# Attention and FFN block on one core: the order of the prologue, and the values matmuls of full-width steps in two halves

## The reference, cut to what matters

```python
sim = jnp.einsum('bhid,bhjd->bhij', q, k)
sim = sim + jnp.transpose(bias, (2, 0, 1)) * SCALE
sim = sim + causal
attn = jax.nn.softmax(sim, axis=-1)
out = jnp.einsum('bhij,bhjd->bhid', attn, v)
```

## Time and profile before

| | us |
|---|---|
| median of 3 runs (lowest to highest) | 344.32 (344.03 to 344.61) |
| the profiled execution | 342.63 |
| its span | 340.8 |
| outside the span | 1.83 |
| TensorE busy | 286.3 |
| VectorE busy | 272.6 |
| ScalarE busy | 190.3 |
| GpSimd busy | 92.0 |

### The profile page before, as it was taken

The page is one execution under the profiler, slowest core; times in us unless marked ns, Lnnn a source line. Parts: engine busy times, 40 slices in busy tenths (PEclk is TensorE's granted clock), DMA queues, the critical chain, the costliest instruction groups (busy, mean ns, idle before and its releaser), DMA issues.

```text
span 340.8 us, 8308 instructions
## 1 busy us (share of the span) xinstructions
PE 286.3 (84%) x3224; PEld 129.0 (38%) x3224; DVE 272.6 (80%) x967; ACT 190.3 (56%) x264; POOL 92.0 (27%) x138
## 2 busy tenths in 40 slices
PE   8492987769998989998898999889899988999880
PEld 4151342222343344334334334423432443367650
DVE  5653556989899888988888989888899957838894
ACT  2433544386558556755766674685575468843230
POOL 6109999602020220201022022001200001615351
PEclk9967698969999999999999999999999999999997
DMA  7475417001010120102022222114221002000022
GB/s 217 131 205 145 132 38 236 17 2 38 21 56 4 56 56 3 53 7 57 0 57 56 34 64 55 35 25 87 56 34 26 9 14 37 4 4 13 0 63 62
DMA packets 16263, 18.80 MB, mean 55 GB/s; under 512 B 4576, under 2 KB 11872, under 8 KB 16096
## 3 DMA queue, kind: packets, MB, share of 16 engines
q1 hardware_dynamic: 13168, 12.10, 14.6%
q0 software_dynamic: 2400, 3.45, 3.5%
q10 hardware_dynamic: 656, 2.73, 2.7%
HBM read 11.81 MB, written 4.23 MB: 47 GB/s over the span
## 4 chain that ended last, share of the span: by engine, by line
PE 52%; DVE 22%; ACT 11%; issue 6%; DMA 4%; POOL 3%; SPq 1%; DVEq 0%; POOLq 0%
PE ps L1174 15%; PE ps L1130 12%; ACT PT L743 9%; DVE FM L883 8%; PE ps L1145 8%; PE ps L1162 7%; DVE junk L890 4%; PE ps L1052 3%; DMA qk_scratch<-QS 2%; PE ps L1207 2%; DVE st L947 2%; DVE U L1000 1%; PE ps L1116 1%; PE ps L1077 1%; DVE xnT L913 1%
## 5 line engine op out<-in xcount | busy, mean ns | idle before, releaser
L743 ACT ACTIVATE PT<-ps 128x1024 f32<-128x1024 f32 (+1 forms) x192 | 144.7, 814 | 92.2 <-PE ps L1162 87.3
L883 DVE TENSOR_REDUCE FM<-ps 128x1 f32<-128x512 f32 (+2 forms) x192 | 109.1, 616 | 12.8 <-PE ps L1130 12.3
L890 DVE CUSTOM_DVE_ANT_0 junk<-ps,NBH 128x256 bf16<-128x256 f32 (+1 forms) x256 | 90.2, 399 | 23.5 <-PE ps L1130 23.5
L1130 PE MATMUL ps<-KA,QA 56*128 56x256 bf16 (+3 forms) x544 | 96.5, 288 | 14.7 <-DVE FM L883 7.4
L1145 PE MATMUL ps<-QA,KA 58*128 58x512 bf16 (+3 forms) x384 | 77.7, 333 | 17.6 <-ACT PT L743 14.6
L1174 PE MATMUL ps<-PT,VG 128*16 128x512 f32 (+3 forms) x768 | 86.1, 493 | 0.1
L1130 PEld LDWEIGHTS ps<-KA,QA 56*128 56x128 bf16 x544 | 33.3, 95 | 99.8 <-DVE FM L883 42.1
L420 POOL DMA_DIRECT2D KA<-qk_scratch x30 | 16.4, 550 | 163.3 <-PE ps L1162 151.9
L1145 PEld LDWEIGHTS ps<-QA,KA 58*128 58x128 bf16 x384 | 24.8, 94 | 37.4 <-ACT PT L743 30.4
L1162 PE MATMUL ps<-TT,flb 128*32 128x176 f16 (+4 forms) x1152 | 38.4, 243 | 0.0
L1162 PEld LDWEIGHTS ps<-TT,flb 128*32 128x32 bf16 x1152 | 21.3, 96 | 17.1 <-issue 15.5
(11 more groups left out here) (98 smaller groups left out, 256.2 us busy)
## 6 DMA issues: line engine op xcount, KB each, us to landing
QA<-qk_scratch SPq DMA_DIRECT2D x64, 48.0 KB
KA<-qk_scratch POOLq DMA_DIRECT2D x30, 96.0 KB, 2.6
qk_scratch<-QS SPq DMA_DIRECT2D x12, 128.0 KB
qk_scratch<-QS SPq DMA_DIRECT2D x8, 192.0 KB
X<-in_x SPq DMA_DIRECT2D x4, 256.0 KB, 5.1
PT<-fr_scratch ACTq DMA_DIRECT2D x1, 1024.0 KB, 5.6
out<-U SPq DMA_DIRECT2D x4, 256.0 KB, 2.3
OT<-f_scratch ACTq DMA_DIRECT2D x2, 480.0 KB, 8.3
```

The source lines that it names most:

```text
L743: nc.scalar.activation(PT[:, s % 3, 2 * q:2 * q + 2, off:off + w], ST[:, q, :, off:off + w], ACT.Exp).then_inc(s_exp, 1)
L883: nc.vector.tensor_reduce(FM[:, ib, heads[0]:heads[-1] + 1:2, piece], bank[:, 0:w * len(heads)].rearrange("p (h n) -> p h n", n=w), AX.X, ...
L890: last = nc.vector.tensor_tensor_reduce(junk[:, n % NSM, i, 0:w], bank[:, i * w:(i + 1) * w], nb[:, h, 256 - w:256], 1.0, NEG, ALU.add, AL ...
L1130: last = nc.tensor.matmul(SM[:, n % NSM, i * w + j - j0:i * w + j - j0 + nj], QA[r0:r0 + KS, p, ib // 4, q, (ib % 4) * 128:(ib % 4 + 1) * ...
```

## The change

- **Bias tables.** `task_f` is split: the reversed table first, its load `rev` issued by SyncE as soon as it is stored; the other table later, its conversion to float16 moved from VectorE to GpSimd, its stores and the TL loads later on SyncE, behind the loads of group 0.
- **Stores.** Query and key stores have semaphores of their own; key parts 1 and 2 of chunk 0 are issued by ScalarE; the third query part of chunk 1 moves from VectorE to GpSimd.
- **TensorE's order.** 10 fillers first (waiting for OV's clearing), F (reversed), T, F (other), Q, K, 5 fillers, V of half 0, 4 fillers, flips 0 to 3, T, Q, K, V of half 1, flips 4 to 7. The banks change with it.
- **Batch 1.** Its eight tasks stand at positions 7, 9, 10, 12, 13, 15, 16, 18 of the unit order, Q and K apart. OWN0 is 21; unit "m 0" of group 0 moves two places forward; the 12 fillers before the first scores go. ScalarE writes Q and K of batch 1 once, GpSimd makes the first part too. The bias copy `copy_tt(0)` is last on ScalarE. GpSimd takes both deviations of batch 1 at once.
- **Values.** A full-width step's values become two halves of 256 columns, with the first unit of the place "after the values" between them.

```diff
+def order_of(g):
+    ks = list(range(NU - 1))
+    if g == 0:
+        ks.remove(M0)
+        ks.insert(M0_FIRST, M0)
+    return ks
+M0_FIRST = SPLIT0 + 3
...
-T_AT = {2: 0, 8: 1}
-QK_AT = {4: 0, 10: 1}
-V_AT = {13: 0, 15: 1}
+BATCH1_AT = {7: ("T", 0), 9: ("Q", 0), 10: ("K", 0), 12: ("V", 0), 13: ("T", 1), 15: ("Q", 1), 16: ("K", 1), 18: ("V", 1)}
-OWN0 = 17
+OWN0 = 21
...
             sp.wait_ge(s_f, 1)
             sp.dma_start(bass.AP(fr_d, 0, [[H, 128], [128 * H, XC], [1, H]]), Fr[:, :, :]).then_inc(s_fst[0], 16)
+            sp.wait_ge(s_fst[0], 16)
+            sp.dma_start(rev[:, :], bass.AP(fr_d, 0, [[H, 128], [1, 256 * H]])).then_inc(s_rev, 16)
+            sp.wait_ge(s_q1, 2)
+            store_keys(sp, 0, 0, 0)
+            store(0, 0, 0)
             sp.wait_ge(s_f, 2)
...
-            key_part(0, 0)
-            key_part(0, 1)
-            store(0, 0, 0)
-            key_part(0, 2)
-            sp.wait_ge(s_qst[0][0], STORED)
+            sp.wait_ge(s_qst[0][0][0], STORED_Q)
             load_q(sp, 0, 0, 0)
...
             load_q(sp, 0, 0, 1)
+            sp.wait_ge(s_fst[1], 32)
+            for part in range(2):
+                sp.dma_start(TL[64 * part:64 * part + 64, :],
+                             bass.AP(f16_d, part * BW * H, [[H, 64], [1, NEARU * H]])).then_inc(s_tl, 16)
...
+            pool.wait_ge(s_ff, 1)
+            nc.gpsimd.tensor_copy(F16[:, 0, :, :], Ff[:, :, :]).then_inc(s_p3, 1)
...
+            queries_lo(0)
             pool.wait_ge(s_zero, 3)
-            pool.wait_ge(s_qst[0][0], STORED)
+            pool.wait_ge(s_p2, 1)
+            pool.wait_ge(s_qst[0][0][1], STORED_K)
             load_k(pool, 0, 0, 0, s_ldk)
-            pool.wait_ge(s_p2, 1)
+            queries_lo(1)
+            second_batch_deviation()
             second_batch_norm(2)
             second_batch_norm(3)
...
+            act.wait_ge(s_mid, 2)
+            store_keys(act, 0, 0, 1)
+            act.wait_ge(s_q3[0][1], 1)
+            store_keys(act, 0, 0, 2)
+            copy_nbh(0)
+            copy_nbh(1)
             turned(0, 1)
-            first_parts(0, 1)
-            for i in NBH_ACT:
+            copy_nbh(2)
+            first_parts(1)
+            for half in range(2):
+                copy_v(0, half)
+            for i in NBH_ACT[3:]:
                 copy_nbh(i)
...
             load_k(act, 0, 0, 1)
-            first_parts(1, 0)
+            whole(0)
+            copy_v(1, 0)
             turned(1, 1)
+            whole(1)
+            copy_v(1, 1)
             act.wait_ge(s_tl, 32)
             copy_tt(0)
-            first_parts(1, 1)
-            copy_v(1)
...
             pe.wait_ge(s_idle, 1)
-            keep_busy(5, 5)
+            pe.wait_ge(s_ov, 2)
+            keep_busy(7, 10)
             pe.wait_ge(s_tab, 16)
-            task_f()
-            keep_busy(5, 2)
+            task_f(1)
             pe.wait_ge(s_early, 16)
             task_t(0, 0)
-            task_qks(0, 0)
-            task_t(0, 1)
-            task_qks(0, 1)
-            pe.wait_ge(s_f, 2)
-            pe.wait_ge(s_ov, 2)
-            pe.wait_ge(s_cst, 2)
+            task_f(0)
+            for qk in range(2):
+                task_qk(0, 0, qk)
+            keep_busy(7, 5)
+            pe.wait_ge(s_mid, 1)
+            task_v(0, 0)
+            keep_busy(7, 4)
+            pe.wait_ge(s_cst, 1)
+            pe.wait_ge(s_ff, 1)
             pe.wait_ge(s_rev, 16)
             for i in range(4):
                 task_flip(i)
...
-            def values(g, p, s):
+            def values(g, p, s, between):
...
-                for h in range(HG):
-                    last = nc.tensor.matmul(OV[32 * h:32 * h + 2 * HD, off:off + w], VG[:, jb, g, h, :],
-                                            PT[:, s % 3, h, off:off + w], start=(jb == 0),
-                                            stop=(jb == 4 * ic + 3), skip_group_check=True)
+                cuts = [(off, w)] if w < IC else [(0, IC // 2), (IC // 2, IC // 2)]
+                for i, (c0, n) in enumerate(cuts):
+                    for h in range(HG):
+                        last = nc.tensor.matmul(OV[32 * h:32 * h + 2 * HD, c0:c0 + n], VG[:, jb, g, h, :],
+                                                PT[:, s % 3, h, c0:c0 + n], start=(jb == 0 and i == 0),
+                                                stop=(jb == 4 * ic + 3), skip_group_check=True)
+                    if i + 1 < len(cuts):
+                        between()
...
-                    values(g, p, s)
-                    s_units_at(s, 2)
+                    early = 1 if step_cols(*STEPS[s])[1] == IC else 0
+                    values(g, p, s, lambda: s_units_at(s, 2, 0, early))
+                    s_units_at(s, 2, early)
...
-            for k in JOBS[:JOBS.index(OWN0)]:
+            for n, k in enumerate(order_of(0)[:OWN0]):
+                if n in BATCH1_AT:
+                    second_batch(*BATCH1_AT[n])
...
             nc.tensor.matmul(ps[0:64, 0, 0:64], flb[:, 0:64], flb[:, 0:64], start=True, stop=True).then_inc(s_pv, 3)
-            keep_busy(1, 12)
             pe.wait_ge(s_tt, 1)
...
-NBH_ACT, NBH_DVE = (0, 2, 4, 5, 6, 7), (1, 3)
+NBH_ACT, NBH_DVE = (0, 1, 2, 4, 5, 6), (3, 7)
```

More of the change, by code:

```diff
@@ L124, in stream @@
     for g in range(G):
-        for k in range(NU - 1):
+        for k in order_of(g):
             if g and k == M1_BEFORE:
@@ L360, in build @@
         s_nbh = sem("s_nbh")
-        s_qst = [[sem(f"s_qst{b}{c}") for c in range(2)] for b in range(B)]
+        s_qst = [[[sem(f"s_qst{b}{c}{x}") for x in "qk"] for c in range(2)] for b in range(B)]
         s_late = sem("s_late")
@@ L863, in _ @@
             norm(1)
-            for k in range(2, 4):
-                stats0(k)
-            for i in NBH_DVE:
-                copy_nbh(i)
+            copy_nbh(NBH_DVE[0])
+            stats0(3)
+            nc.vector.tensor_copy(idb[:, :], idf[:, :]).then_inc(s_cst, 1)
             for qk in range(2):
                 split(1, qk)
+            copy_nbh(NBH_DVE[1])
             def unit(g, p, k):
@@ L1035, in _, with task_f @@
         def _(pe):
-            def task_f():
-                for k in range(2 * XC):
-                    last = nc.tensor.matmul(ps[:, BANK["F", 0, 0], k * H:(k + 1) * H],
-                                            oh_s[:, k // XC, (k % XC) * 128:(k % XC + 1) * 128], emb_s[:, :],
+            def task_f(a):
+                for c in range(XC):
+                    last = nc.tensor.matmul(ps[:, BANK["F", 0, a], c * H:(c + 1) * H],
+                                            oh_s[:, a, c * 128:(c + 1) * 128], emb_s[:, :],
                                             start=True, stop=True)
@@ L1095, in _ @@
             pe.wait_ge(s_mid, 2)
-            task_v(0, 0)
+            task_t(0, 1)
+            for qk in range(2):
+                task_qk(0, 1, qk)
             task_v(0, 1)
@@ L1226, in group, with s_units_at @@
             def group(g, p, load, last=False, first=False):
-                def s_units_at(s, pos):
-                    for later, k in (SLOTS0 if first else SLOTS).get((s, pos), []):
+                def s_units_at(s, pos, i0=0, i1=None):
+                    for later, k in (SLOTS0 if first else SLOTS).get((s, pos), [])[i0:i1]:
                         if later and last:
@@ L1307, in stage0_tasks @@
 def stage0_tasks():
[L1309 removed]
+    order = [("F", 0, 1), ("T", 0, 0), ("F", 0, 0), ("Q", 0, 0), ("K", 0, 0), ("V", 0, 0),
+             ("T", 0, 1), ("Q", 0, 1), ("K", 0, 1), ("V", 0, 1)]
     for half in range(2):
[L1311 to L1317 removed]
+        order += [(kind, 1, half) for kind in "TQKV"]
+    bank = {("F", 0, 1): 6, ("F", 0, 0): 5}
+    bank.update({("T", 0, 0): 0, ("T", 0, 1): 3, ("Q", 0, 0): 2, ("K", 0, 0): 3, ("Q", 0, 1): 4,
                  ("K", 0, 1): 5, ("V", 0, 0): 2, ("V", 0, 1): 3,
```

183 lines of the change are left out of this document (90 added, 93 removed).

## The result

The changed kernel takes 340.81 us in the median of 4 runs (337.59 to 341.20), beside 344.17 for the kernel before on the same chip (342.29 to 344.61). The ratio is 0.9882, with a 95% interval of 0.9840 to 0.9924: faster by 1.2%, some 4 us by the ratio (3.4 by the medians), where 12 were forecast. The profiled execution took 341.2 us, its span 339.4.

What follows compares the result with a forecast made beforehand. Prologue held to be bound by waits, chiefly an 8.36 us key and query landing, steady groups by TensorE's chain with excursions through VectorE. -10.0 (A) and -2.0 (B) take 344.32 to 332.3 us; range 324.5 to 340.

Steps and rivals of the forecast that it cites:

- part B: Values of full-width steps in two halves with a unit between: -0.3 us per group, -2 us in all, bounds +8 and -13.
- part A: The prologue, up to the end of group 0: reordered loads and units save 10.0 us, bounds 3 and 14.
- below 2.5: Sign that the forecast is right: VectorE's idle time in a steady group of 28.9 us falls under 2.5 us.
- Step (1): Start of the units: key parts land at 20.0 us instead of 25.35, units start at 25.3; -5.4 us, bounds -1.3 and -6.9.
- The other gate: Start of the units: the bias tile is ready near 24.5 us, just hidden behind the loads; 1 us of delay shows.
- Step (2): First unit to first scores: 13.0 us of VectorE work and 4.6 idle, 17.6 in all, bounds 15 and 20.4.
- only part of A arrives: Rival, 20%: in the prologue a queue takes back what the DMA gave; A -4, B about 0, 340 us.
- The normalised tile comes 4 to 5 us earlier: Units to first scores: GpSimd's batch 1 tile comes earlier with the key load, so TensorE's 2.1 us wait goes.
- the fillers' 2.70 us: Units to first scores: the 12 filler matmuls are removed and their 2.70 us go.
- Step (3): Rest of group 0: VectorE work falls by 2.6 us, a low clock may cost some; -1.8 us, bounds -4 and +1.
- takes about twice that: Rest of group 0: without fillers, one full-width block of 0.99 us takes about twice as long at the low clock.
- slower: Rival, 8%: in steps 5 to 8 the unit between values waits for its bank; at 2.0 us per group, +13, 345.5 us.

Runs made afterwards that it cites:

- e1: The changed kernel with the values of full-width steps in one piece again, so the prologue part alone: 341.19 us, ratio 0.9916 to the kernel before.
- e4: The changed kernel with values in halves but no unit between them, the units behind as before: 341.76 us, ratio 0.9899 to the kernel before.
- e12: The changed kernel itself, unaltered, measured once more on one chip beside later runs: 339.75 us, ratio 0.9859 to the kernel before.
- e11: e8 with two fillers ahead of each of nine units in step 2 of group 0: 331.95 us, ratio 0.9620 to the kernel before.
- e3: The changed kernel with SyncE's TL loads, and what stands behind them, waiting for the chunk 1 keys and queries: 337.56 us, ratio 0.9783 to the kernel before.
- e9: The changed kernel, order of loads left alone, with both sets of fillers of e8: 339.17 us, ratio 0.9845 to the kernel before.
- e8: e5 with the fillers of both e6 and e7: 331.17 us, ratio 0.9591 to the kernel before.
- e6: e5 with 10 filler matmuls ahead of the first unit and 2 ahead of each of units 1 to 6: 332.81 us, ratio 0.9670.
- e7: e5 with 8 filler matmuls ahead of the first scores: 333.00 us, ratio 0.9651 to the kernel before.
- e5: e3 with the maximum row sent ahead of group 1's first query loads, and GpSimd's key loads moved behind batch 1's splits: 335.87 us, ratio 0.9724.
- e10: e8 with the values in one piece, the edit of e1: 334.57 us, ratio 0.9714 to the kernel before.

## Why the prediction was wrong

The direction was right (faster, 90%) and so was part B. The size of part A was wrong by 7 us (2.9 in e1, where 10 had been forecast, just outside its own bounds of 3 to 14), and 340.81 lies outside the range, though only just above it.

**Part B**, forecast -0.3 us per group. It is -0.43: 28.74 for 29.17, and five periods between the same output copies (107.16 to 250.86 against 106.72 to 252.55) give 2.1 us. The turn back from a unit costs 0.1 (0.32 for 0.22), as put, and the mechanism was the one named: ScalarE's exponentials start earlier once the unit does, and VectorE's gap closes in part. Part of the gap stays (0.18 here); the idle time in a group is 2.59 us, just missing the "below 2.5". The Trainium skill's rule that a change of the tiling mode drains TensorE (TensorEngine Tiling (Array Packing), Key Properties) bears on the turns alone: the trace shows their price and not what they consist of, and e4, which cuts without a unit between, costs nothing.

**Step (1)**, units at 25.3 us, forecast -5.4. The landing of the key parts fell from 8.36 to 5.00 us (4.4 in e12), where 4.26 had been put. But the part was ready at 16.60 instead of 15.68: Q and K start at 10.12, X having landed after 4.17 us and the other table (1.46 us) standing ahead of them, and they took 3.78 us in spite of the ten fillers. Units start at 27.55, and between 25.4 and 27.6 in all profiles with this prologue but that of e11 (29.53). The other gate was near, as said: the bias tile is ready at 25.11, and in e3 it releases the first unit. So 3 to 5 of the 5.4 came.

**Step (2)**, 17.6 us from units to first scores, is the step that failed: it took 24.1 us (26.6 in e12). VectorE's work was 13.11 as forecast (13.0), so the idle time was mis-sized, 11 us against 4.6. Three terms of it:

- "The change puts the two loads of the diagonal bias (480 KB each) behind everything of group 0" is true of SyncE's queue alone. The key load of chunk 1 is ScalarE's, and ScalarE comes to it 0.75 us after SyncE is past. I had read the order of one queue as the order of the loads. It costs a landing of 7.12 us where e3 shows 2.5 or less, and, by e3, 2 to 3 us of the time; and by e9 the fillers give nothing that can be told before it is mended. The rival "only part of A arrives" (20%), with 4 us left of A and 340 us in all, came nearest, though its B was put at nothing. It named GpSimd's norm behind the key load, which is one half of this (next point), and not ScalarE's key load beside the TL loads.
- "The normalised tile comes 4 to 5 us earlier": it comes 1.5 earlier (31.70 for 33.22, the start of its transpose), since GpSimd passes its wait for the key parts at 22.14 instead of 20.0, and the operation added ahead of the norm costs 1.17. This is what makes ScalarE late for its key load; e9 shows that being 0.8 us earlier would not have been enough.
- The clock. Only the rest of group 0 had a term for it. The first half's Q and K of batch 1 take 2.05 and 2.08 us as before at the low level, and the second half's 1.95 and 1.13, where the earlier trace rows has both in 1.96. In e8 each of the four takes 1.10 to 1.13. The forecast counted the fillers' 2.70 us as gained, and nothing for the clock that they had kept up; on the mended order, e8 puts that at 4.6 us and e6 and e7 at 2 to 3 each.

That the bias copy shows by about 1 us before the first scores came true (1.55).

**Step (3)**, -1.8. "Its VectorE work falls by the same 2.6" came true (-2.4), yet the stretch to the row's transfer shrank by 0.5. The mean clock over it is 0.62; with eight fillers back ahead of the scores (e7), first scores to first output copy fall from 23.5 us (e5) to 20.9. That a full-width block at the low clock "takes about twice that" was about the right price (half a block, eight records, takes 1.05 us at 59.60 and 0.62 at 145.46), and was counted at one block where it holds for most of 54 to 62 us and 68 to 80 us.

**The size of the whole** was not out of reach: e8, with the two queues ordered and the fillers in, takes 331.17 us, where 332.3 was forecast, and e10, its prologue without part B, is worth 9.9 us where part A was put at 10.0. That the sizes agree is in part luck: the forecast had counted the fillers as time saved, and e8 has 30 of them. It had priced the change that was meant and not the one that was made.

A slip beside this: the rival *slower* has 345.5 "with A at -12". The forecast's A is -10, and 344.3 - 12 + 13 is 345.3; with A at -10 it is 347.3. Its sign and chance do not hang on it.

What stays open: the clock term of the changed kernel is shown by adding fillers, not by a run at another clock; what makes the keys land late, the 960 KB alone or also the loads of group 1 issued behind them, is not parted; and the 3 us between the first scores and the output copy of e7 and e6 (20.9 and 23.9) were not looked into by engine.

## What to carry to other kernels

When a big load is moved later, write down every queue's issues with their expected times, not only those of its own queue: a small load that another engine issues at about the same time shares its way with it, and landed 5 us later here, which cost 2 to 3 us of the kernel. To issue it a little earlier is no cure: 0.07 us ahead it was as late (e9). Put a wait in front of the big load on the thing that it must not overtake, and put small transfers on the critical path ahead of the loads of the next stage. Fillers in the stretches where TensorE waits paid here only after the wait that comes last there was gone (e8 against e9), and where their own time was idle anyway (e8 against e11). A unit of work for a second engine that stands between two long blocks can be put into the middle of one, when its bank is free there; the cut itself was free (e4).

## What the runs showed of the hardware

- The same key load, four parts of chunk 1, landed in 7.12, 7.46 and 7.91 us with 960 KB put out at about the same time (from 0.07 us behind its first part to 0.75 us ahead of it), and in 2.5 us or less when those were held back (e3); and the small transfer of the maximum row in 6.51 us instead of 1.8 behind such loads (e3). A transfer issued from another engine is not shielded from them. The Trainium skill (DMA: Bandwidth & Descriptors, Issuing engines are not separate DMA queues) says that transfers of several issuing engines run on the same DMA engines and interleave, and these landings agree; the prediction had used the rule for the stores and not for the loads.
- The granted clock was 0.50 from 26 to 38 us of the changed kernel and 1.00 in e8, and each Q or K there took 2.05 to 2.08 and 1.10 to 1.13 us. But the column doesn't explain every slow matmul: Q and K of half 0 take 3.78 us both in the changed kernel, where 10 to 14 us is granted at 0.50, and in e8, where the same stretch reads 1.00; the same four records take 1.98 us at 19.34 in e8. In the first 14 us I go by the duration and not by the column; no run here shows why they differ. Busy time by stretch of e8:

```profile
10.00:14.00 4.00, 4.00 (x6) 1.50 (x7) 2.36 (x11) 0.80 (x2) 0.85 (x3) 1.00 0.68 262
```
